# A fused AdaLN and ternary FFN kernel: the residual is read from DRAM a second time instead of being copied by ScalarE, and the input load moves to the top of the chunk

## The chip, the cores and the metric

The kernel runs on one core of a Trainium2 chip. The metric is the device time of one execution in microseconds, lower is better. Beside it stands the span of the profiled execution, which reaches from the first to the last instruction of the core.

## What is computed

```python
# conditional mixing of channels: per sample b an own 64 x 64 matrix
h = gelu(cond @ W0 + b0); h = gelu(h @ W1 + b1)
att = softmax(h @ W2 + b2)
agg_w = einsum('bk,koi->boi', att, weight); agg_b = att @ bias_k
y = einsum('boi,bih->boh', agg_w, x) + agg_b[:, :, None]
# feed-forward with ternary weights q(w) * mean|w|
gate = y @ deq(w_gate).T; up = y @ deq(w_up).T        # 1024 -> 2752
out = x + (gate * up) @ deq(w_down).T                 # 2752 -> 1024
```

x is 64 x 64 x 1024 in float32, that is 4096 tokens of 1024 values. The last line adds x itself: this is the residual.

## The kernel before

The 4096 tokens are worked through in eight chunks of 512 tokens, numbered 0 to 7. Chunk 0 runs together with the preparation of the weights (scales, ternary values, transposes, and the sums of weight blocks that a Strassen-like scheme needs, which are stored to DRAM as `wcomb`, `dcomb` and `wsub`). Chunks 1 to 7 follow one pattern. Chunk 1 (`FIRST`) and chunk 7 are written out, chunks 2 to 6 are a loop on each engine.

A chunk has eleven steps `p` on TensorE (`pairs`), each of which computes two 128-row blocks of gate and up as seven block products P1 to P7 (L971). In chunks 2 to 7, P2 and P5 are split once more (`inner_a` to `inner_d`, L983) and use extra weights, 128 KB for each of the two, that SyncE loads from `wsub` into `hi_r`/`sub` and `g_r` (`sub_load`, L603). Step 0 has only the first of the two. Twice in a chunk a group of down projections runs (`down_group`, L1089): group 0 before step 6, group 1 at the end. VectorE adds each of their banks, scaled, to `xr` (`output2`, L2016), which must hold the residual by then. After the last addition SyncE stores `xr` to the output (`store2`, L645), 256 KB at a time.

Within steps 2 to 5 of chunk c the input of chunk c+1 is mixed: `conv(c + 1, k)` (L742), two at a step, read `xa`, the 2 MB of x of chunk c+1, against `ablk`, the block-diagonal mixing matrices. The first of them stands in step 2, behind P1, `inner_a`, P4 and `inner_b`.

All loads of a chunk are issued from one queue, SyncE's, in a fixed order. SyncE runs down this list, and a wait stops all that is behind it:

```python
def chunk(c):
    if inners(c, 2):
        sub_third(c)          # waits for P2 of step 0, then loads the wsub blocks of step 2
    next_x(c)                 # ablk, xa and bias of chunk c+1
    pairs(c)                  # ring loads of wcomb (L597) and wsub blocks for the later steps
    next_pairs(c)
    store2(c)
    sp.wait_ge(s_dn, ...)
    down_load(0)              # 2240 KB of dcomb for the next chunk (L624)
```

`xr` gets its residual from ScalarE: `residual(c, t)` (L1219) copies a quarter of `xa` to `xr`, two quarters in step 0 and two in step 1, behind the copies of P1 and P6 that these steps need. Since `xa` may be overwritten only after that, `next_x` waits for all four copies (`s_xr`) besides the end of the chunk's own `conv` (`s_y`). The bias of chunk c+1 is loaded behind `xa`, 256 KB, one row spread over all partitions.

Of the kernel before, what the change touches and what calls it, by code (L numbers as in the profile page):

```python
# [5 lines left out]
def adaln_ternary_ffn(nc: bass.Bass, x, cond, w0, b0, w1, b1, w2, b2, wk, bias_k, w_gate, w_up, w_down, out):  # L6
# [15 lines left out]
    NT = TOK // P  # L22
    NC = B * C // TOK
# [7 lines left out]
    HB = H // TOK  # L31
# [59 lines left out]
    def sum_count(i):  # L91

        return on_act[i], sum((on_act if on_act[i] else on_dve)[:i + 1])
# [69 lines left out]
    with ctx:  # L163
        def sb(name, shape, dt):
            return ctx.enter_context(nc.sbuf_tensor(name, shape, dt))

        def sem(name):
            return ctx.enter_context(nc.semaphore(name))
# [9 lines left out]
        xa = sb("xa", [P, NT, H], f32)  # L178
        xr = sb("xr", [P, NT, H], f32)
# [212 lines left out]
        def inners(c, p):  # L392

            if isinstance(c, int) and c == FIRST or p == NPR:
                return ()
            return INNER[0:1 if p == 0 else NI]
# [46 lines left out]
        s_t = sem("s_t")  # L443
        s_te = sem("s_te")
        s_x = sem("s_x")
        s_xr = sem("s_xr")
        s_ablk = sem("s_ablk")
        s_bb = sem("s_bb")
        s_bbv = sem("s_bbv")
# [61 lines left out]
        s_res = [sem(f"s_res{t}") for t in range(NT)]  # L511
# [10 lines left out]
        s_st = [sem(f"s_st{t}") for t in range(NT)]  # L522

        xt = x.rearrange("(t b) c h -> t (b c) h", b=2)
# [6 lines left out]
        def _(sp):  # L531
            for dst, src in ((cond_sb, cond), (w0_sb, w0), (b0_sb, b0[:, None])):
                sp.dma_start(dst, src).then_inc(s_cond, 16)
            def load_x(c):

                sp.dma_start(xa[:, :, :], xt[bass.ds(c * NT, NT), :, :].rearrange("t p h -> p t h")).then_inc(s_x, 16)
# [8 lines left out]
            def load_bias(c):  # L545
                sp.dma_start(bbc[:, :], bias_row(c)).then_inc(s_bias, 16)

            last_in = {}
            for e, (n, _, _, s) in enumerate(loads):
                if e == 2:  # L550
                    load_x(0)
                if s in last_in:
# [3 lines left out]
                    else:  # L556
                        act, count = sum_count(summed.index(last_in[s]))
# [20 lines left out]
            sp.wait_ge(s_bst, 16)  # L578
            load_bias(1)

            def next_x(c):
                sp.wait_ge(s_xr, NT * c)
                sp.wait_ge(s_y, KH * c + KH)
                if isinstance(c, int) and c == FIRST:
                    sp.wait_ge(s_ad, 16)
                for h in range(2):
                    sp.dma_start(ablk[h * C:(h + 1) * C, :, h * C:(h + 1) * C],  # L587
                                 aggd[h * C:(h + 1) * C, bass.ds((c + 1) * NT, NT), :]).then_inc(s_abd, 16)
                load_x(c + 1)
                sp.wait_ge(s_ysc, KH * c + KH)  # L590
                load_bias(c + 1)
# [9 lines left out]
            def sub_load(c, p):  # L601
                for q, _ in enumerate(inners(c, p)):
                    sp.dma_start(sub_ring[q][p % 2], wsub[p, q]).then_inc(s_sub[p % 2], 16)  # L603

            def sub_third(c):
                sp.wait_ge(s_m2, NS * (c - FIRST) + 1)
                sub_load(c, 2)

            def next_pairs(c):
                if isinstance(c, int) and c == FIRST:  # L610
                    sp.wait_ge(s_subd, NI * NPR)
                for p, before in ((0, NPR - 1), (1, NPR), (2, NPR - 2)):
                    sp.wait_ge(s_m3, NS * (c - FIRST) + before + 1)
                    ring_load(p)
                if isinstance(c, int) and c == FIRST:
                    for i in range(2):
                        sp.wait_ge(s_subw[i], 16 * NI * (NPR // 2))
                sp.wait_ge(s_ulo, UP * FIRST + 2 * (c - FIRST) + 1)
                sub_load(c + 1, 0)
                sub_load(c + 1, 1)  # L620

            def down_load(g):
                dst = wd_flat[:, 0:GRP * PART].bitcast(f32).rearrange("p (q n) -> p q n", q=GRP)
                sp.dma_start(dst, dcomb[g * GRP:(g + 1) * GRP].rearrange("q p n -> p q n")).then_inc(s_wd, 16)  # L624

            def pairs(c):
                for p in range(RING, NS):
                    if p > RING and inners(c, p - 1):
                        sp.wait_ge(s_done[INNER[-1]], NS * (c - FIRST) + p - 2)
                        sub_load(c, p - 1)  # L630
                    sp.wait_ge(s_m3, NS * (c - FIRST) + p - RING + 1)
                    if isinstance(c, int) and c == FIRST:
                        sp.wait_ge(s_subd, NI * (p - RING + 1))
                    ring_load(p)
                    if p == NPR:
                        sp.wait_ge(s_dn, DN * FIRST + ND2 * (c - FIRST) + len(DOWN[0]))
                        down_load(1)

            def store2(c):
                for d, (what, j) in enumerate(DOWN[1]):  # L640
                    if d >= len(QUADS):
                        t, n = OUT[what][0] + j, OUT[what][1]
                        sp.wait_ge(s_o, DN * FIRST + ND2 * (c - FIRST) + len(DOWN[0]) + d + 1)
                        sp.sem_inc(s_turn_sp, 1)
                        sp.dma_start(ot[c * NT + t, :, n * TOK:(n + 1) * TOK],  # L645
                                     xr[:, t, n * TOK:(n + 1) * TOK]).then_inc(s_st[t], 16)
# [11 lines left out]
            down_load(0)  # L658

            def chunk(c):  # L660
                if inners(c, 2):
                    sub_third(c)
                next_x(c)
                pairs(c)
                next_pairs(c)
                store2(c)
                sp.wait_ge(s_dn, DN * FIRST + ND2 * (c - FIRST) + ND2)
                down_load(0)

            chunk(FIRST)  # L670
            with sp.Fori(FIRST + 1, NC - 1) as c:
                chunk(c)
            sub_third(NC - 1)
            pairs(NC - 1)
            store2(NC - 1)
# [520 lines left out]
        def _(act):  # L1196
# [15 lines left out]
                act.wait_ge(s_ysc, n + 1)  # L1212
                nc.scalar.copy(yp[:, k, 0, :], ys[:, k, :]).then_inc(s_yhi, 1)

            def residual(c, t):

                act.wait_ge(s_x, 16 * (c + 1))
                act.wait_ge(s_st[t], 16 * HB * c)
                nc.scalar.copy(xr[:, t, :], xa[:, t, :]).then_inc(s_xr, 1)  # L1219

            def raw_sum(i):
                e = summed[i]
                n = loads[e][0]
# [235 lines left out]
            def inner2(c, p):  # L1459
                n = len(inners(c, p))  # L1460
                act.wait_ge(s_ib, NPR * (c - FIRST - 1) + p + 1)
                nc.scalar.copy(uppers[:, 0:n, 0, :], lowers[:, 0:n, 0, :]).then_inc(s_e2, 1)
# [23 lines left out]
            def pairs(c, more):  # L1486
                for p in range(NS):
                    copy_p1(c, p)
                    if inners(c, p):
                        inner1(c, p)  # L1490
                    elif p < 2:
                        residual(c, 2 * p)
                        residual(c, 2 * p + 1)
                    if p:
                        gate21(c, p - 1)
                    if inners(c, p):
                        inner2(c, p)
                        inner3(c, p)
                    copy_p16(c, p)
                    if inners(c, p) and p < 2:  # L1500
                        residual(c, 2 * p)
                        residual(c, 2 * p + 1)
                    if more and p - 2 in range(KH // 2):
                        magnitudes(c + 1, 2 * (p - 2))
                        magnitudes(c + 1, 2 * (p - 2) + 1)
                    if p:
                        hi_blocks(c, p - 1)
                    copy_p167(c, p)
                    if p:
                        hi_sums(c, p - 1)  # L1510
                hi_rest(c)
                act.wait_ge(s_last, c - FIRST + 1)
                nc.scalar.copy(f_last[0], blocks4[0][:, 0:TOK]).then_inc(s_uhi, 1)
                if more:
                    hi_quarters(c + 1)
# [8 lines left out]
        def _(dve):  # L1524
# [476 lines left out]
            def output2(c, g, d):  # L2001
                done = DN * FIRST + ND2 * (c - FIRST) + g * len(DOWN[0])
                what, j = DOWN[g][d]
                t, n = OUT[what][0] + j, OUT[what][1]
                bank = DBANK[g][CHAIN[what]][j]
                dve.wait_ge(s_dn, done + d + 1)
                if g == 0 and d == 0:
                    dve.wait_ge(s_xr, NT * c)
                    dve.wait_ge(s_osc, c + 1)
                same = [e for e, (a, b) in enumerate(DOWN[g][:d]) if (OUT[a][0] + b, OUT[a][1]) == (t, n)]  # L2010
                if same:
                    dve.wait_ge(s_o, done + same[-1] + 1)
                elif g:
                    dve.wait_ge(s_o, done)
                cols = slice(n * TOK, (n + 1) * TOK)
                V.scalar_tensor_tensor(xr[:, t, cols], bank[:, :], osc[:, t:t + 1], xr[:, t, cols],  # L2016
                                       ALU.mult, ALU.add).then_inc(s_o, 1)
# [114 lines left out]
```

## Time and profile before

| | |
|---|---|
| median of 3 runs | 1733.4 us (1732.54 to 1737.3) |
| profiled execution | 1732.3 us, span 1730.3 us |
| TensorE busy | 1694.4 us, 98% of the span |
| VectorE busy | 1178.6 us, 68% |
| ScalarE busy | 682.1 us, 39% |
| mean granted TensorE clock | 0.995 |
| DRAM read, written | 176.63 MB, 34.68 MB |

Busy time counts only instructions that compute. The profiled execution took 2.0 us more than its span. The granted clock is the share of full speed that TensorE got: 1.00 is 2.4 GHz and 0.50 is 1.2 GHz.

### The profile page before, as it was taken

To read this page: it belongs to the slowest core of one execution; us is meant where nothing else is said; L and a number is where in the kernel's file an instruction comes from. 1 tells how busy PE (TensorE), PEld (TensorE's weight loads), DVE (VectorE), ACT (ScalarE), POOL (GpSimd) and SP (SyncE) were. 2 spreads that over 40 slices of the span, in tenths; PEclk is the share of its full clock that TensorE was granted. 3 is DMA by queue.
4 is the path that set the end of the run, shared out by engine and by line. 5 is a ranking of instruction groups with operands and counts; after the bars stand their busy time and mean duration, and the time that the engine had idled before them with its cause. 6 is when DMAs were issued, how large, how long until landed. Compare 5 with 4: busy or idle time off the path is not lost.

```text
span 1730.3 us, 35263 instructions
## 1 busy us (share of the span) xinstructions
PE 1694.4 (98%) x13784; PEld 1220.3 (71%) x13792; DVE 1178.6 (68%) x1960; ACT 682.1 (39%) x1281; POOL 89.3 (5%) x148
## 2 busy tenths in 40 slices
PE   6999999999999999999999999999999999999999
PEld 5554545977768686795957968587776868679594
DVE  6898895675766758566684766857576675766464
ACT  6887742322334234341433414343242423434140
POOL 0010004342000000000000000000000000000000
PEclk9999999999999999999999999999999999999999
DMA  8667626411333132430325302342133411332121
GB/s 342 248 243 254 215 104 224 141 62 50 143 111 139 56 114 86 166 106 28 120 104 169 103 31 104 120 164 83 51 142 110 141 56 58 136 136 93 40 99 49
DMA packets 80529, 213.62 MB, mean 123 GB/s; under 512 B 10704, under 2 KB 25616, under 8 KB 80240
## 3 DMA queue, kind: packets, MB, share of 16 engines
q1 hardware_dynamic: 76112, 193.23, 31.6%
q0 software_dynamic: 3664, 18.03, 2.7%
q8 instruction: 117, 1.92, 0.4%
q14 instruction: 44, 0.36, 0.1%
q10 hardware_dynamic: 592, 0.09, 0.0%
HBM read 176.63 MB, written 34.68 MB: 122 GB/s over the span
## 4 chain that ended last, share of the span: by engine, by line
PE 93%; DMA 3%; SPq 2%; ACT 1%; DVE 1%; issue 1%; ACTq 0%; DVEq 0%
PE ps L971 39%; PE ps L1089 25%; PE ps L742 17%; PE ps L983 10%; DMA xa<-in_x_dram 2%; PE ps L1048 2%; SPq L565 1%; DMA wuT<-in_L_ffn_w_gate_dram 1%; PE ps L848 1%; ACT xr L1219 1%; SPq L587 0%; DVE msk L1673 0%; DVE xa L1744 0%; DVE prod L1711 0%; ACT wdT L1282 0%
## 5 line engine op out<-in xcount | busy, mean ns | idle before, releaser
L971 PE MATMUL ps<-yp,wgT 128*128 128x256 f16 x3204 | 718.7, 273 | 1.0 <-issue 0.9
L971 PE MATMUL ps<-wuT,wgT 128*128 128x256 f16 x3204 | 718.5, 273 | 0.0
L1089 PE MATMUL ps<-wdT,inter 128*128 128x512 fp8e4 x1960 | 434.2, 379 | 0.5 <-DVE l L1610 0.2
L1089 PEld LDWEIGHTS ps<-wdT,inter 128*128 128x128 f16 x1960 | 191.3, 98 | 226.9
L971 PEld LDWEIGHTS ps<-yp,wgT 128*128 128x128 fp8e4 x3204 | 314.6, 98 | 38.7 <-issue 2.9
L971 PEld LDWEIGHTS ps<-wuT,wgT 128*128 128x128 fp8e4 x3204 | 314.5, 98 | 36.4
L2016 DVE SCALAR_TENSOR_TENSOR xr<-ps,osc,xr 128x512 f32<-128x512 f32 x210 | 156.9, 748 | 126.5 <-PE ps L1089 102.3
L1421 ACT COPY raw<-ps 128x512 f32<-128x512 f32 (+1 forms) x77 | 43.6, 567 | 307.3 <-PE ps L971 307.0
L1934 DVE TENSOR_TENSOR wdT<-ps,msk 128x512 f32<-128x512 f32 (+1 forms) x77 | 51.4, 667 | 78.9 <-PE ps L971 78.9
L742 PE MATMUL ps<-ablk,xa 128*128 128x128 f32 x512 | 71.9, 288 | 17.3 <-DMA xa<-in_x_dram 16.9
L1999 DVE TENSOR_TENSOR inter<-inter 128x1024 f16<-128x1024 f32 x70 | 85.3, 1218 | 0.0
L1943 DVE TENSOR_TENSOR ps<-p,ps 128x256 f32<-128x256 f32 x114 | 43.6, 426 | 56.7 <-ACT ps L1469 56.7
L742 PEld LDWEIGHTS ps<-ablk,xa 128*128 128x128 f32 x512 | 65.1, 200 | 20.3 <-issue 17.6
L1381 ACT CAST yp<-ys 128x1024 f16<-128x1024 f32 x49 | 48.4, 1042 | 72.7 <-DVE ys L1827 44.1
L742 PE MATMUL ps<-yp,wgT 128*128 128x512 f16 x336 | 76.0, 379 | 0.0
L983 PE MATMUL ps<-wuT,wgT 128*128 128x128 f16 x456 | 75.4, 219 | 0.0
L983 PE MATMUL ps<-yp,wgT 128*128 128x128 f16 x456 | 75.4, 219 | 0.0
L742 PE MATMUL ps<-yp,wuT 128*128 128x512 f16 x336 | 75.1, 379 | 0.0
L742 PE MATMUL ps<-wdT,inter 128*128 128x512 fp8e4 x336 | 73.8, 379 | 0.0
L1451 ACT CAST inter<-inter 128x1024 f16<-128x1024 f32 x70 | 73.4, 1048 | 0.0
L1435 ACT COPY raw<-ps 128x512 f32<-128x512 f32 (+1 forms) x77 | 43.5, 564 | 65.6 <-PE ps L971 65.6
L1443 ACT COPY inter<-ps 128x256 f32<-128x256 f32 x70 | 26.0, 372 | 107.6 <-PE ps L971 107.6
(273 smaller groups left out, 2311.7 us busy)
## 6 DMA issues: line engine op xcount, KB each, us to landing
wgT<-wcomb SPq DMA_DIRECT2D x70, 896.0 KB, 4.8
wdT<-dcomb SPq DMA_DIRECT2D x14, 2240.0 KB, 8.9
xa<-in_x_dram SPq DMA_DIRECT2D x8, 2048.0 KB, 8.5
out_dram<-xr SPq DMA_DIRECT2D x64, 256.0 KB, 2.0
wcomb<-xa POOLq DMA_DIRECT2D x17, 448.0 KB, 3.0
g_r<-wsub SPq DMA_DIRECT2D x54, 128.0 KB, 4.3
xr<-in_L_ffn_w_down_dram SPq DMA_DIRECT2D x9, 512.0 KB, 6.0
hi_r<-wsub SPq DMA_DIRECT2D x30, 128.0 KB, 3.6
```

The costliest lines, as they stand in the source:

```text
L742: return nc.tensor.matmul(o, l, r, start=start, stop=stop)
L971: last = nc.tensor.matmul(out, w, operand(i, OPERAND[what])[:, k, :], start=(start and h + k + i == 0), stop=(k == KQ - 1 and i == 1), ski ...
L983: last = nc.tensor.matmul(out, wk, inner_x(what, i, x)[:, k, :], start=(start and k + i == 0), stop=(k + i == 2), skip_group_check=True)
L1089: last = nc.tensor.matmul(bank[:, :], x, wd_block(p, BLOCK[what]), start=(what in ("P1", "P2", "P5") and q + i == 0), stop=(q == GRP - 1 a ...
L1381: nc.scalar.copy(operand(0, s), quarter(s)).then_inc(s_yhi, 1)
L1421: nc.scalar.copy(t1[:, 0:w], PB[p % 2][:, 0:w]).then_inc(s_t1, 1)
L1435: nc.scalar.copy(q67[:, 0:w], PB[p % 2][:, 0:w]).then_inc(s_q67, 1)
L1451: nc.scalar.copy(pair_parts(p, 0, 3, 4), sums).then_inc(s_hiS, 1)
L1934: V.tensor_tensor(rr[:, 0:w], PC[p % 2][:, 0:w], q6[p % 2][:, 0:w], ALU.add).then_inc(s_c12, 1)
L1943: last = V.tensor_tensor(inner_bank(p, what)[:, HALF:TOK].rearrange("p (a n) -> p a n", a=2), uppers[:, q], lowers[:, q, 1].unsqueeze(1).b ...
L1999: V.tensor_tensor(pair_parts(p, 1, 3, 4), sums, pair_parts(p, 0, 3, 4), ALU.subtract).then_inc(s_loS, 1)
L2016: V.scalar_tensor_tensor(xr[:, t, cols], bank[:, :], osc[:, t:t + 1], xr[:, t, cols], ALU.mult, ALU.add).then_inc(s_o, 1)
```

## The change

ScalarE's copies and their semaphore are removed. A new `load_res(c)` on SyncE's queue loads the same four quarters, 512 KB each, from x in DRAM to `xr`, each after the stores of that quarter of the chunk before have landed (`s_st[t]`). VectorE's outputs of group 0 wait for that load (`s_res[t]`). `next_x` loses the wait for the copies. `next_x` and `load_res` stand at the top of the chunk, ahead of `sub_third`. In chunk 7, which has no next chunk, only `load_res` is added, also ahead of `sub_third`.

```diff
+            def load_res(c):
+                for t in range(NT):
+                    sp.wait_ge(s_st[t], 16 * HB * c)
+                    sp.dma_start(xr[:, t, :], xt[c * NT + t]).then_inc(s_res[t], 16)
+
             def next_x(c):
-                sp.wait_ge(s_xr, NT * c)
                 sp.wait_ge(s_y, KH * c + KH)
...
             def chunk(c):
+                next_x(c)
+                load_res(c)
                 if inners(c, 2):
                     sub_third(c)
-                next_x(c)
                 pairs(c)
...
             with sp.Fori(FIRST + 1, NC - 1) as c:
                 chunk(c)
+            load_res(NC - 1)
             sub_third(NC - 1)
...
-            def residual(c, t):
-
-                act.wait_ge(s_x, 16 * (c + 1))
-                act.wait_ge(s_st[t], 16 * HB * c)
-                nc.scalar.copy(xr[:, t, :], xa[:, t, :]).then_inc(s_xr, 1)
...
                     if inners(c, p):
                         inner1(c, p)
-                    elif p < 2:
-                        residual(c, 2 * p)
-                        residual(c, 2 * p + 1)
...
                     copy_p16(c, p)
-                    if inners(c, p) and p < 2:
-                        residual(c, 2 * p)
-                        residual(c, 2 * p + 1)
...
                 if g == 0 and d == 0:
-                    dve.wait_ge(s_xr, NT * c)
                     dve.wait_ge(s_osc, c + 1)
...
                 elif g:
                     dve.wait_ge(s_o, done)
+                else:
+                    dve.wait_ge(s_res[t], 16 * (c + 1))
```

## Rows read from the trace of the kernel before

**Rows 1.** The page's chain that ended last, by engine and by line.

```profile
PE 93%; DMA 3%; SPq 2%; ACT 1%; DVE 1%; issue 1%; ACTq 0%; DVEq 0%
```

**Rows 2.** Waits of TensorE, whole span: total us, times, longest us.

```profile
PE ps L742 <- DMA xa<-in_x_dram: 16.9, 6, 3.8
```

**Rows 3.** The chain that ended last, 720 to 741 us (chunk 3): start us, us, what.

```profile
721.60 2.00 ACT xr L1219 x2
723.62 0.05 SPq L583
...
725.55 8.26 DMA xa<-in_x_dram
733.81 0.12 issue
733.93 1.58 PE ps L742 x8
...
739.82 1.75 PE ps L971 x16
```

**Rows 4.** The same chain, chunk 5, from its first input mixing on.

```profile
1149.12 1.15 PE ps L742 x8
...
1153.36 1.75 PE ps L971 x16
```

**Rows 5.** Busy time by stretch, chunk 3; last three columns: granted clock, DMA share, GB/s.

```profile
712.00:713.00 1.00, 1.00 (x14) 0.92 (x12) 0.65 (x1) 1.00 (x2) 0.00 (x0) 1.00 1.04 413
720.00:721.00 1.00, 1.00 (x13) 0.91 (x11) 0.68 (x3) 0.70 (x3) 0.00 (x0) 1.00 0.00 0
732.00:733.00 1.00, 0.00 (x0) 0.00 (x0) 0.37 (x2) 0.00 (x0) 0.00 (x0) 1.00 1.01 416
735.00:736.00 1.00, 1.00 (x7) 0.75 (x6) 0.13 (x1) 0.00 (x0) 0.00 (x0) 0.50 0.99 388
```

**Rows 6.** SyncE's DMA issues in order of time, chunk 3: start us, us.

```profile
706.40 0.43 SPq L624 DMA_DIRECT2D wdT<-dcomb  x1
712.34 0.33 SPq L603 DMA_DIRECT2D hi_r<-wsub  x1
...
723.89 1.48 SPq L587 DMA_DIRECT2D ablk<-aggd  x2
725.55 0.82 SPq L536 DMA_DIRECT2D xa<-in_x_dram  x1
726.57 0.35 SPq L546 DMA_DIRECT2D bbc<-biasd  x1
726.97 0.43 SPq L597 DMA_DIRECT2D wgT<-wcomb  x1
```

**Rows 7.** DMA issues of 700 to 740 us: count, KB each, us from issue to landing.

```profile
wdT<-dcomb SPq DMA_DIRECT2D x1, 2240.0 KB, 9.0
xa<-in_x_dram SPq DMA_DIRECT2D x1, 2048.0 KB, 8.3
wgT<-wcomb SPq DMA_DIRECT2D x1, 896.0 KB, 11.2
...
bbc<-biasd SPq DMA_DIRECT2D x1, 256.0 KB, 9.3
```

**Rows 8.** TensorE in order of time, first matmul of `inner_a` in step 2, chunk 3.

```profile
727.50 0.22 PE L983 MATMUL ps<-yp,wgT 128*128 128x128 f16 x1
```

**Rows 9.** The same two points of chunk 2, the issue of `dcomb` and that matmul.

```profile
499.39 0.43 SPq L624 DMA_DIRECT2D wdT<-dcomb  x1
...
520.12 0.22 PE L983 MATMUL ps<-yp,wgT 128*128 128x128 f16 x1
```

**Rows 10.** Start of the kernel: SyncE's issues, then busy time by stretch.

```profile
3.97 1.98 SPq L565 DMA_DIRECT2D wdT<-in_L_ffn_w_gate_dram  x3
10.38 7.08 SPq L565 DMA_DIRECT2D inter<-in_L_ffn_w_gate_dram  x7
...
8.00:24.00 16.00, 15.48 (x97) 13.38 (x98) 9.99 (x23) 9.90 (x20) 0.00 (x0) 1.00 1.02 409
```

**Rows 11.** Groups by line, ScalarE's copies: count, busy us, mean ns, idle before.

```profile
L1219 ACT COPY xr<-xa 128x1024 f32<-128x1024 f32 x28 | 27.9, 1048 | 0.0
```

**Rows 12.** VectorE in order of time, the first output of group 0 in chunk 3.

```profile
789.11 0.74 DVE L2016 SCALAR_TENSOR_TENSOR xr<-ps,osc,xr 128x512 f32<-128x512 f32 x1
```

More of the change, by code:

```diff
@@ L445, in adaln_ternary_ffn @@
         s_x = sem("s_x")
-        s_xr = sem("s_xr")
         s_ablk = sem("s_ablk")
```

## Prediction

> **What bounds the kernel now.** I read the page's chain of work that ended last first: TensorE holds 93% of it, DMA 3%, SyncE's queue 2% and ScalarE 1% [rows 1]. So the kernel is bound by TensorE's own work, and only time in which TensorE stands still or runs at half clock can be won. The list of TensorE's waits comes next. Its largest entry is the first input mixing, which waited for `xa` six times, 16.9 us in all, 3.8 us at most [rows 2]. Five of these are large, one in each of chunks 2 to 6 (3.4, 3.2, 3.8, 3.3 and 3.0 us in the waits of each chunk's stretch, sum 16.7 us); chunks 1 and 7 have none.
>
> The chain in order of time tells why `xa` is late. In chunk 3 ScalarE's last two residual copies run from 721.6 to 723.6 us, then SyncE's wait for them ends, it issues `ablk`, and at 725.55 us `xa`, which takes 8.26 us; the mixing starts at 733.93 us [rows 3]. Meanwhile the DMA engines were idle: 0 GB/s at 720 us [rows 5]. So the load is late because of its wait, not because the engines were full.
>
> The stall has a second price. After it the granted clock is 0.50 (1.2 GHz), where it was 1.00 (2.4 GHz) before and during most of it [rows 5]. From the first mixing to the end of the second, chunk 3 takes 739.82 - 733.93 = 5.89 us, chunk 5, which kept its full clock behind a like stall, 1153.36 - 1149.12 = 4.24 us [rows 3, 4]: 1.65 us lost. The same difference in chunks 4 and 6 is 1.65 us and in chunk 2 it is 1.37 us. Slow clock costs 3 x 1.65 + 1.37 = 6.3 us. All that the late `xa` costs is then 16.7 + 6.3 = 23.0 us.
>
> **The change part by part.**
>
> *Copies removed.* 28 copies of 1048 ns, 27.9 us [rows 11], leave ScalarE. It is no releaser of TensorE in any chunk from 1 to 7, so I take 0 from this. Bounds: 0 and, if the two copies of a step in chunk 1 hid a wait behind P6, a gain of about 2 us.
>
> *Wait removed and load moved.* `next_x` now runs behind `down_load(0)`, issued at 706.40 us in chunk 3 [rows 6]. From the end of SyncE's wait to the issue of `xa` it took 725.55 - 723.62 = 1.9 us [rows 3], so `xa` is issued near 708.9 us instead of 725.55. It is queued behind the 2240 KB of `dcomb`, which land 9.0 us after their issue [rows 7], that is at 715.4 us. With 5.1 us of transfer it is in by about 721.5 us, and the mixing wants it near 730.6 us (733.93 minus the 3.2 us stall and the release). The old stall goes, and its slow clock with it: a gain of 23.0 us if nothing else comes late.
>
> *What is now ahead of `sub_third`.* This is the step that decides. `sub_third` loads what `inner_a` of step 2 reads. Before, it was issued at 712.34 us [rows 6], as soon as P2 of step 0 was done, right behind `dcomb`, and had some 12 us to spare before 727.50 us [rows 8]. Now four residual loads (2048 KB in all), `xa` (2048 KB), `ablk` and the bias stand ahead of it, in one queue whose transfers land in the order of issue. I add up how long the queue needs, from the issue of `dcomb`:
>
> - `dcomb`: 9.0 us to landing, of which about 0.8 us is `sub_third`'s own data, which ran beside its tail: 8.2 us.
> - `ablk`: 128 KB in rows of 256 bytes. Before, it ran within the 1.48 us of its issues [rows 6]; 0.3 us (by bytes at 413 GB/s [rows 5]) to 2.0 us. I take 1.2.
> - `xa`: 2048 KB at 413 to 416 GB/s [rows 5] is 5.1 us. Upper bound 7.5 us, at the mean rate of `dcomb` (2.29 MB in 8.2 us, 280 GB/s).
> - bias: it landed at 726.57 + 9.3 = 735.9 us, `xa` at 725.55 + 8.3 = 733.9 us [rows 6, 7]: 2.0 us. Lower bound 0.7 us by bytes.
> - residual: 2048 KB as `xa`: 5.1 us, up to 7.5.
> - `sub_third`: 256 KB, 0.9 us; before, the like pair landed about that much behind the ring load at 726.97 + 11.2 = 738.2 us [rows 6, 7].
>
> Sum 22.5 us. `inner_a` starts 727.50 - 706.40 = 21.1 us after that issue in chunk 3 and 520.12 - 499.39 = 20.7 us in chunk 2 [rows 6, 8, 9]. With a mean need of 20.95 us and 0.12 us for the release [rows 3] the new stall is 1.7 us a chunk, five times: 8.5 us. Bounds: the low ends give 8.2 + 0.3 + 5.1 + 0.7 + 5.1 + 0.7 = 20.1 us, no stall; the high ends 8.2 + 2.0 + 7.5 + 2.0 + 7.5 + 0.9 = 28.1 us, a stall of 7.3 us. SyncE itself is no limit. The start of the kernel shows what it does with a long backlog: its issues of 512 KB grow from 0.66 to 1.0 us each while 409 GB/s move [rows 10]. An issue held up there is still served in turn.
>
> The rate of 413 to 416 GB/s is read from single microseconds and 409 GB/s from sixteen in a row [rows 5, 10]. The Trainium skill (DMA: Bandwidth & Descriptors, section Bandwidth) speaks against such a rate: it says that for transfers between HBM and SBUF the HBM side, about 358 GB/s a core, is what binds. By it the two 2 MB loads would take some 1.7 us more together, and the stall would be about 3.4 us. This trace does not agree with it, so my sum goes by the rows.
>
> *The clock behind the new stall.* I take no slow clock for a wait of 1.7 us. The rows show it behind waits of 3.0 us and more, and not even behind each of them [rows 3, 4]. Bounds: 0 and 1.65 us each, 8.2 us.
>
> *Chunks 1 and 7.* Chunk 1 has no `sub_third`. In chunk 7 the queue holds `dcomb` and the residual alone, 8.2 + 5.1 + 0.9 = 14.2 us against 21: nothing. The ring load of step 3 waits for P3 of step 0, near 722.7 us, and would land at about 731.5 us; before it landed at 738.2 us and nobody waited.
>
> *VectorE's new wait.* The residual is in by 728 us, and the first output of group 0 comes at 789.11 us [rows 12]. Cost 0, with 60 us of cover. The loads add 14.7 MB of DRAM traffic. Beyond its place in the queue I cost it at 0: TensorE was busy for all of the microsecond in which 413 GB/s moved [rows 5].
>
> Sum: 16.7 + 6.3 - 8.5 = 14.5 us less. The profiled execution took 1732.3 us, so 1717.8 us, and the median of the runs is 1.1 us above it: 1718.9 us.
>
> **The rivals.**
>
> *No new stall.* The queue drains a little faster than I add up, or `ablk` and bias overlap with their neighbours. Then all 23.0 us are won: 1710.4 us. For it: I am only 1.6 us over the need, and the two small loads, 3.2 us of my sum, move 0.9 us worth of bytes. Against it: the bias really held the queue for 2.0 us before.
>
> *The stall only changes its name.* The wait at `inner_a` is as long as the old one and slow clock follows as before. That needs the queue to take about 24.3 us, 1.8 us more than my sum, which loads at 350 GB/s give. Then 23.0 us are won and 5 x 3.4 + 6.3 = 23.3 us lost: 1733.7 us. It is in this mechanism that the rule above has its place, with that result.
>
> *Slower.* The queue runs at `dcomb`'s mean rate of 280 GB/s for the big loads, as two streams from x follow each other without a gap. At the high ends it takes 28.1 us, the stall is 7.3 us, and each is followed by slow clock: 5 x (7.3 + 1.65) = 44.8 us against 23.0, so 1755 us. It decides from 24.4 us on. For it: `dcomb` needed about 2 us to come up to full rate. Against it: that is a start, and the sustained rate in a long backlog was 409 GB/s [rows 10].
>
> *The change doesn't do what it says.* If `next_x` were held at the top by its other wait (`s_y`, done a chunk earlier), nothing would move. I see no way for this, and fold it into the case of no change.
>
> **How the numbers follow.** Chances: stall of 0.5 to 3 us moved to `inner_a`, 0.50; no stall, 0.20; the stall only renamed, 0.14; slower, 0.16. A measurement of this kernel can tell about 0.3%, 5 us. The likeliest case has its own range: a stall of 0.5 us gives 23.0 - 2.5 = 20.5 us and one of 3 us without slow clock 8 us, so 1713 to 1725 us. With the no-stall case below it and the renamed stall above it the range is 1709 to 1735 us, which leaves out the slower case. Faster by over 0.3%: 0.50 + 0.20 + 0.03 of the third = 0.73; within it 0.12; slower 0.15.
>
> **What would show it.** In the profile after: no wait of L742 for `xa`; `xa` issued within 3 us of `dcomb`; in chunks 2 to 6 a wait of L983 in step 2 for a `wsub` load, 1 to 2 us long, whose issue-to-landing time has grown from 3 us to 12 or more; mean granted clock nearly 1.00; no L1219. If the wait is over 3.4 us or the clock still falls, the sum of the queue is wrong and the time goes to 1733 us or beyond; if L983 never waits, it is 1710 us. A wait of VectorE at the first output of group 0 would break my claim of cover.

## The result, and the profile after

The changed kernel takes 1718.42 us in the median (1715.75 to 1721.8, 4 runs), the kernel before 1735.35 us beside it (1732.54 to 1737.93). The ratio is 0.9904, with a 95% interval of 0.9878 to 0.9930: faster, by 17 us. The forecast was 1718.9 us, a ratio of 0.9916 to the 1733.4 us of the section before. The profiled execution took 1718.81 us, span 1716.8 us, mean granted clock 0.997.

The first views are the page's shares of the chain that ended last, and below them the list of TensorE's waits (total us, times, longest us).

```profile
PE 90%; DMA 5%; SPq 2%; DVE 1%; issue 1%; ACT 1%; DVEq 0%; ACTq 0%
...
PE ps L988 <- DMA g_r<-wsub: 7.2, 5, 2.0
PE ps L752 <- DMA inter<-in_L_cond_b_dram: 4.2, 1, 4.2
PE ps L747 <- ACT msk L1236: 3.0, 1, 3.0
```

Where [rows 2] had 16.9 us of waiting for `xa`, the list has one wait of 0.3 us left, ahead of chunk 1. In its place stands a wait of the product matmuls for `g_r`, one of the two `wsub` blocks of step 2: five times, 7.2 us, once in each of chunks 2 to 6 (1.7, 1.4, 2.0, 1.2 and 0.9 us by each chunk's stretch). That is the new stall that the prediction put at 1.7 us a chunk. The DMA share of the chain went up from 3% [rows 1] to 5% although the kernel got faster: a chain credits the whole time of the load that released it, here some 15 us each, and not the wait alone.

SyncE's issues in chunk 3, in order of time (start us, us), answer to [rows 6]:

```profile
704.40 0.43 SPq L627 DMA_DIRECT2D wdT<-dcomb  x1
705.54 1.46 SPq L590 DMA_DIRECT2D ablk<-aggd  x2
707.18 0.47 SPq L535 DMA_DIRECT2D xa<-in_x_dram  x1
707.87 1.38 SPq L545 DMA_DIRECT2D bbc<-biasd  x1
709.52 1.92 SPq L583 DMA_DIRECT2D xr<-in_x_dram  x4
711.59 0.55 SPq L606 DMA_DIRECT2D hi_r<-wsub  x1
712.18 1.63 SPq L606 DMA_DIRECT2D g_r<-wsub  x1
720.63 0.37 SPq L600 DMA_DIRECT2D wgT<-wcomb  x1
```

`xa` is issued 2.8 us after `dcomb` instead of 19.2 us. The chain in order of time shows what became last instead (start us, us, what):

```profile
712.18 14.53 DMA g_r<-wsub
726.71 0.14 issue
726.85 1.05 PE ps L988 x16
```

The 128 KB of `g_r` were issued 7.8 us after `dcomb`, 1.5 us later than before, but need 14.53 us. They land 726.71 - 704.40 = 22.3 us after the issue of `dcomb`; the sum of the prediction was 22.5 us. Busy time by stretch (last three columns: granted clock, DMA share, GB/s) shows why: from 708 us on the DMA engines never paused.

```profile
708.00:714.00 6.00, 6.00 (x68) 5.50 (x67) 2.66 (x5) 1.70 (x4) 0.00 (x0) 1.00 1.00 374
715.00:720.00 5.00, 5.00 (x57) 4.57 (x55) 2.28 (x6) 2.04 (x6) 0.00 (x0) 1.00 1.02 401
721.00:726.00 5.00, 4.43 (x49) 3.80 (x46) 4.54 (x9) 2.90 (x4) 0.00 (x0) 1.00 1.04 398
```

The queue can be taken apart by its landings. These are the same issues of chunk 3 with KB and us from issue to landing (the second `ablk` load, issued at 706.39 us, and the last of the four `xr` loads, issued at 711.11 us):

```profile
wdT<-dcomb SPq DMA_DIRECT2D x1, 2240.0 KB, 9.6
ablk<-aggd SPq DMA_DIRECT2D x1, 64.0 KB, 8.4
xa<-in_x_dram SPq DMA_DIRECT2D x1, 2048.0 KB, 12.9
bbc<-biasd SPq DMA_DIRECT2D x1, 256.0 KB, 13.0
xr<-in_x_dram SPq DMA_DIRECT2D x1, 512.0 KB, 15.0
hi_r<-wsub SPq DMA_DIRECT2D x1, 128.0 KB, 13.2
```

Added to the starts above, `dcomb` lands 9.6 us after its issue, `ablk` at 10.4 us, `xa` at 15.7 us, the bias at 16.5 us, the last residual quarter at 21.7 us and `g_r` at 22.3 us. The order of landing is that of issue but for small loads: `hi_r`, issued behind all of the residual, landed at 20.4 us, 1.3 us ahead of its last quarter.

Slow clock came after one of the five waits, in chunk 4: this is its granted clock shortly behind the wait.

```profile
933.00:934.00 1.00, 1.00 (x6) 0.71 (x5) 0.00 (x0) 0.21 (x2) 0.00 (x0) 0.50 0.03 9
```

### The profile page after: what moved, and what is told of

Its sections match the earlier page's. It is cut to its first block, busy times and chain, and to the rows that moved or that the text cites. A ratio compares the mean times of both kernels' runs of the same rounds, so it can differ in the third digit from the quotient of the medians.

```text
span 1716.8 us, 35301 instructions
## 1 busy us (share of the span) xinstructions
PE 1692.5 (99%) x13792; PEld 1218.2 (71%) x13792; DVE 1178.6 (69%) x1960; ACT 656.3 (38%) x1253; POOL 90.5 (5%) x148
## 4 chain that ended last, share of the span: by engine, by line
PE 90%; DMA 5%; SPq 2%; DVE 1%; issue 1%; ACT 1%; DVEq 0%; ACTq 0%
PE ps L976 36%; PE ps L1094 25%; PE ps L747 18%; PE ps L988 9%; DMA g_r<-wsub 4%; PE ps L1053 2%; PE ps L853 1%; DMA xa<-in_x_dram 1%; SPq L583 0%; SPq L545 0%; SPq L590 0%; ACT msk L1236 0%; DVE xr L2010 0%; SPq L535 0%; DVE msk L1666 0%
## 5 line engine op out<-in xcount | busy, mean ns | idle before, releaser
L1911 DVE TENSOR_TENSOR wdT<-ps,raw 128x512 f32<-128x512 f32 (+1 forms) x77 | 51.3, 666 | 24.2 <-ACT raw L1434 24.2
```

Source lines behind the costliest of these rows:

```text
L1911: V.tensor_tensor(rr[:, TOK - w:TOK], PC[p % 2][:, 0:w], q67[:, 0:w], ALU.add).then_inc(s_c22, 1)
```

## The experiments

Each was run beside the kernel before on one chip, and its ratio is to that. "Wait" is TensorE's own wait for DMA in chunks 1 to 6 of the profiled execution.

**1. The wsub load first.** If only the order in the queue makes the new wait, putting this load back at the head must remove it, with all the rest of the change kept.

```diff
             def chunk(c):
-                next_x(c)
-                load_res(c)
                 if inners(c, 2):
                     sub_third(c)
+                next_x(c)
+                load_res(c)
...
+            sub_third(NC - 1)
             load_res(NC - 1)
-            sub_third(NC - 1)
```

> The changed kernel with the wsub load of step 2 back at the head of the chunk, and the input load and the residual loads behind it. Theory A (the stall of 7.2 us that the changed kernel shows at the first product of step 2 comes only from what stands ahead of that load in the queue): the input load is issued some 6 us later than in the changed kernel but still lands near 18 us after the chunk begins, before its use at 24 us; no wait of TensorE in chunks 2 to 6, no slow clock there, 7 to 9 us less than the changed kernel, about 1710 us and a ratio of 0.985 to the kernel before. Theory B (the queue as a whole carries too much, whatever the order): a wait of 1 to 2 us a chunk appears at the first input mixing or at the ring load of step 3 instead, 1718 us, ratio 0.990.

Measured: 1709.38 us (1707.79 to 1711.34), ratio 0.9865, interval 0.9846 to 0.9883. SyncE's issues in chunk 3, and the top of the list of waits, which holds no DMA wait of any chunk but the one at the start of the kernel:

```profile
702.28 0.97 SPq L627 DMA_DIRECT2D wdT<-dcomb  x1
708.63 0.33 SPq L606 DMA_DIRECT2D hi_r<-wsub  x1
...
711.38 0.98 SPq L535 DMA_DIRECT2D xa<-in_x_dram  x1
```

```profile
PE ps L752 <- DMA inter<-in_L_cond_b_dram: 4.2, 1, 4.2
PE ps L747 <- ACT msk L1236: 3.0, 1, 3.0
PE ps L747 <- DVE l L1617: 2.0, 1, 2.0
```

`xa` lands 8.6 us after its issue, at 720.0 us, and its first use comes at 726.88 us: it can afford being issued 9.1 us after `dcomb` instead of 2.8. Theory A holds, B falls.

**2. The residual loads alone behind the wsub load.** Here the input load stays at the top. The part left out swaps the two loads of chunk 7, as above.

```diff
             def chunk(c):
                 next_x(c)
-                load_res(c)
                 if inners(c, 2):
                     sub_third(c)
+                load_res(c)
...
```

> The changed kernel with the residual loads behind the wsub load of step 2, the input load still at the top. Theory A (the four residual loads, 5.1 us of queue, are what made the wsub load late): it lands near 17 to 18 us after the dcomb issue instead of 22.5, before its use at 21, so no wait, as in the version with the wsub load first; 1709 to 1710 us, ratio 0.9865. Theory B (the input load, ablk and bias ahead are enough): 1 us or more of wait a chunk stays, 1714 us or more.

Measured: 1709.66 us (1708.41 to 1710.17), ratio 0.9867 (0.9853 to 0.9882), and no wait either. The slowest `g_r` load of the kernel now takes 11.1 us from issue to landing instead of 15.1 us. In chunk 3, start us and us of the two issues, then KB and us from issue to landing of the second:

```profile
703.30 0.53 SPq L627 DMA_DIRECT2D wdT<-dcomb  x1
...
709.50 0.43 SPq L606 DMA_DIRECT2D g_r<-wsub  x1
```

```profile
g_r<-wsub SPq DMA_DIRECT2D x1, 128.0 KB, 10.8
```

It lands 17.0 us after `dcomb` was issued, 5.3 us earlier than in the changed kernel, where 2 MB more stood ahead of it. So the residual ahead was what made the load late: theory A holds, B falls.

**3. A longer queue.** The opposite: 512 KB more ahead of the wsub load.

```diff
...
                 load_res(c)
+                if not isinstance(c, int):
+                    sp.wait_ge(s_spare, 16 * (c - FIRST))
+                sp.dma_start(spare_x, xt[c * NT]).then_inc(s_spare, 16)
                 if inners(c, 2):
                     sub_third(c)
```

> The changed kernel with 512 KB more in SyncE's queue ahead of the wsub load of step 2: a quarter of x is copied once more, from DRAM to a DRAM tensor that nobody reads. Theory A (the stall is the time that the queue needs, whatever is in it): the wait grows by the time of those bytes, 1.3 us at 410 GB/s, up to 2.6 us if a copy within DRAM counts twice, so from 1.5 to about 2.8 to 4 us a chunk, 14 to 20 us in all, with slow clock behind some; 1725 to 1734 us, ratio 0.994 to 1.000. Theory C (the stall comes from the issue of the wsub load by SyncE, not from the queue behind it): the issue is only 0.5 us later, so 2 to 3 us more in all, ratio 0.992.

To have it beside the changed kernel on one chip, that was run again too:

> The changed kernel itself, unchanged, so that the three that follow can be compared with it on one chip. Theory A: ratio 0.990, a wait of 1 to 2 us at the first product of step 2 in each of chunks 2 to 6, 7 to 8 us in all.

Measured: the changed kernel 1720.09 us (1719.34 to 1725.37), ratio 0.9937 (0.9922 to 0.9951), wait 8.2 us; with the longer queue 1730.75 us (1726.29 to 1736.31), ratio 0.9990 (0.9977 to 1.0002), wait 14.7 us. The list of TensorE's waits, first of the changed kernel run again, then of the longer queue:

```profile
PE ps L988 <- DMA g_r<-wsub: 8.2, 5, 2.0
```

```profile
PE ps L993 <- DMA g_r<-wsub: 14.7, 5, 4.0
```

(14.7 - 8.2) / 5 = 1.3 us a chunk, and 512 KB at 400 GB/s take 1.3 us. The wait grew by the time of the added bytes (theory A), and a copy within DRAM counted once. This run alone doesn't rule out theory C, since SyncE also issued `g_r` later, 9.0 us after `dcomb` instead of 7.8 us. Experiment 2 does: there `g_r` was issued 6.2 us after `dcomb`, as early as in the kernel before (6.3 us), and yet took 10.8 us to land where it had taken 4.0 us, with `xa`, `ablk` and bias ahead of it. The medians differ by 10.7 us, of which the waits are 6.5; the profiled spans (1725.3 and 1717.4 us) by 7.9 us, with one more stretch of slow clock, about 1.7 us. A further 512 KB thus ate most of what the change had won.

**4. The bias out of the way.** The prediction gave the 256 KB bias load 2.0 us, more than its bytes.

```diff
                 load_x(c + 1)
-                sp.wait_ge(s_ysc, KH * c + KH)
-                load_bias(c + 1)
...
                 if inners(c, 2):
                     sub_third(c)
+                sp.wait_ge(s_ysc, KH * c + KH)
+                load_bias(c + 1)
```

> The changed kernel with the 256 KB bias load taken from ahead of the residual loads and put behind the wsub load of step 2. Theory A as in the prediction (the bias holds the queue for 2.0 us): the wait at the first product of step 2 falls by 2.0 us a chunk, to nothing in most, 1711 to 1713 us, ratio 0.987 to 0.989. Theory D (in a full queue the bias runs beside its neighbours and takes about 0.7 us): the wait falls by 0.7 us a chunk, to about 0.8 us, 1714 to 1717 us, ratio 0.990 to 0.992.

Measured: 1718.22 us (1712.34 to 1720.72), ratio 0.9909 (0.9892 to 0.9927), and in the list of waits:

```profile
PE ps L988 <- DMA g_r<-wsub: 3.1, 5, 0.8
```

That is 0.6 us a chunk, against 1.4 in the profile of the changed kernel and 1.6 in its second one: the bias took 0.8 to 1.0 us, near theory D's 0.7 us and not 2.0. The landings of the changed kernel say the same: in chunk 3 the bias came 0.8 us behind `xa`. The whole time is wide here. The profiled execution had a span of 1710.4 us and is the fastest of the runs, 6 us under their median, so the whole time can't weigh the two sizes and only the waits and landings do.

**5. The input load late again.** The copies stay removed and the residual comes from DRAM, but the input load is held back to where ScalarE's last copy had let it go.

```diff
             def chunk(c):
-                next_x(c)
-                load_res(c)
                 if inners(c, 2):
                     sub_third(c)
+                load_res(c)
+                sp.wait_ge(s_c12, NS * (c - FIRST) + 1)
+                next_x(c)
...
```

> The changed kernel with the wsub load and the residual loads first, and the input load held back until VectorE's addition for P3 of step 0, which ends close to where ScalarE's last residual copy ended in the kernel before. ScalarE's copies stay removed and the residual still comes from DRAM. Theory A (the lateness of the input load was what cost time): the input load is issued near 19 us into the chunk as before, TensorE waits about 3 us a chunk for it, 16 us in all, with slow clock behind most, and the time is that of the kernel before, 1733 us, ratio 0.997 to 1.002. Theory B (taking the copies off ScalarE gave part of the gain): ratio 0.993 to 0.996.

Measured: 1739.14 us (1733.78 to 1741.6), ratio 1.0037 (1.0023 to 1.0051). TensorE's waits, and the chain in chunk 3 as far as the mixing:

```profile
PE ps L748 <- DMA xa<-in_x_dram: 19.1, 7, 3.4
```

```profile
726.95 0.70 DVE wdT L1928
...
729.93 7.84 DMA xa<-in_x_dram
737.77 0.12 issue
737.89 1.15 PE ps L748 x8
```

`xa` is issued 19.3 us after `dcomb`, as in the kernel before (19.2 us). The whole gain is gone, though the copies are off ScalarE and the residual comes from DRAM. It is even 7 us worse than before, more than theory A's range allowed. 3.4 us of that are a wait in chunk 1, which this version holds back as well and which had none before. The profiled execution is the fastest of the ten and can't show the rest, but the mean granted clock of each run can: in the median 0.992 here and 0.995 for the kernel before beside it, which is about 5 us of 1735 us by my estimate. Theory A's mechanism holds, theory B falls.

**6. ScalarE's work put back.** Filler copies, as long as the removed ones and at their places.

```diff
...
+            def filler(c, p):
+                for i in range(7):
+                    if not (isinstance(c, int) and c == FIRST and p + i == 0):
+                        act.wait_ge(s_idle, 14 * (c - FIRST) + 7 * p + i)
+                    nc.scalar.copy(idle[:, :], ones[:, :]).then_inc(s_idle, 1)
...
+                    elif p < 2:
+                        filler(c, p)
...
                     copy_p16(c, p)
+                    if inners(c, p) and p < 2:
+                        filler(c, p)
```

> The changed kernel with as much copying put back on ScalarE as was removed, at the same places: 28 blocks' worth, seven copies of 128 x 128 for each two of the old ones, about 2.2 us each time, from a constant to a tile that nobody reads. Theory A (the copies cost nothing by themselves): same time as the changed kernel, within 2 us, ratio 0.990, and the waits of TensorE unchanged. Theory B (ScalarE's relief is part of the gain): 3 us or more slower than the changed kernel, with waits of TensorE for ScalarE in steps 0 and 1.

> The kernel with the filler copies on ScalarE once more, now on the same chip as the changed kernel. Theory A (the copies cost nothing by themselves; the 2.8 us more that it showed on another chip lie in the spread of the stall from execution to execution): within 3 us of the changed kernel. Theory B (they cost something): 3 us or more slower than it again.

Measured: 1721.21 us, ratio 0.9931 (0.9913 to 0.9948), and the second time, beside the changed kernel's 1720.09 us and 0.9937 (0.9922 to 0.9951), 1721.77 us and 0.9946 (0.9932 to 0.9960). The fillers were 98 copies of 299 ns, 29.3 us busy. No wait of TensorE for ScalarE appeared in steps 0 and 1; the waits for `g_r` were 8.5 and 9.0 us. The first time the kernel was 2.8 us slower than the changed kernel on another chip, on one chip 1.7 us. The intervals overlap: these runs show no cost of ScalarE's copies by themselves, but with four to six runs each they leave room for a few us. Experiment 7 narrows it.

**7. The kernel before, with the copies earlier.** If the late release was everything, the second read from DRAM is not needed at all. In chunks 2 to 7 ScalarE now makes two copies behind the copy of P6 and two behind that of P7, all in step 0.

```diff
                     copy_p16(c, p)
-                    if inners(c, p) and p < 2:
-                        residual(c, 2 * p)
-                        residual(c, 2 * p + 1)
+                    if inners(c, p) and p == 0:
+                        residual(c, 0)
+                        residual(c, 1)
...
                     copy_p167(c, p)
+                    if inners(c, p) and p == 0:
+                        residual(c, 2)
+                        residual(c, 3)
```

> The kernel before, with one thing changed: in chunks 2 to 7 ScalarE makes all four residual copies in step 0, two behind the copy of P6 and two behind the copy of P7, instead of two in step 1. No DRAM re-read, and SyncE's order is that of the kernel before. Theory A (only the late release of the input load cost time): the release comes at about 11 us into the chunk instead of 18, the input load lands near 21 to 22 us, its use is at 25 us, so the stall is gone, and with the wsub load of step 2 ahead no other takes its place: 20 to 23 us less than the kernel before, about 1713 us, ratio 0.987. Theory B (the DMA engines must have the second read in place of the copies to gain): little change, ratio 0.997 or more, and TensorE waits for ScalarE in step 1, whose copy of P1 comes late.

Measured: 1709.71 us (1708.5 to 1710.05), ratio 0.9865 (0.9845 to 0.9885). ScalarE in chunk 3, then SyncE's issues behind it:

```profile
707.34 0.59 ACT L1428 COPY msk<-ps 128x512 f32<-128x512 f32 x1 [0.44 <-PE ps L971]
707.82 2.00 ACT L1219 COPY xr<-xa 128x1024 f32<-128x1024 f32 x2
710.63 0.59 ACT L1435 COPY raw<-ps 128x512 f32<-128x512 f32 x1 [0.81 <-PE ps L971]
711.11 1.99 ACT L1219 COPY xr<-xa 128x1024 f32<-128x1024 f32 x2
713.00 0.59 ACT L1421 COPY raw<-ps 128x512 f32<-128x512 f32 x1
```

```profile
713.40 1.48 SPq L587 DMA_DIRECT2D ablk<-aggd  x2
715.06 0.47 SPq L536 DMA_DIRECT2D xa<-in_x_dram  x1
```

`xa` lands 7.8 us later, at 722.8 us, and is used from 727.12 us on. No wait remains in the chunks. Theory A holds, B falls. This version was run again beside the first experiment's on one chip:

> The kernel before with all four copies of ScalarE in step 0, once more, beside the next one on one chip: no wait of TensorE in chunks 2 to 7, 1709 to 1710 us, ratio 0.9865.

> The changed kernel with the wsub load of step 2 first, once more, beside the version above on one chip. Its 14.7 MB of additional DRAM reads are hidden, so the two should lie within 2 us of each other, 1709 to 1710 us, ratio 0.9865.

Measured: 1710.15 us (1708.5 to 1710.67), ratio 0.9862 (0.9843 to 0.9880), and 1708.61 us (1708.41 to 1709.61), ratio 0.9858 (0.9840 to 0.9876). The two can't be told apart, and each beats both kernels. One of them has ScalarE's copies and the other the second read of x from DRAM, so the two cost the same within about 2 us. Against the kernel before, these four measurements win 22.3 to 24.8 us, and 23.0 us was all that the late `xa` was put at, which leaves little for a cost of either.

## Why the prediction was right

*What bounds the kernel.* Right: the late input load cost a wait in chunks 2 to 6, and nothing else that the change removes mattered. Experiment 5 gives the gain back by that one delay. Experiment 7 wins 22.3 and 23.2 us by that one release, where all that the late `xa` costs was put at 23.0 us.

*Copies removed: 0.* Right within some 2 us (experiments 5, 6 and 7).

*The moved load: all of the old stall.* Right. No wait for `xa` is left in chunks 1 to 7, and the 16.7 us of waiting are gone.

*The queue ahead of `sub_third`.* The deciding step was right in kind and in its sum, 22.5 us forecast and 22.3 us measured, and the stall, 8.5 us forecast, was 7.2 us in one profile and 8.2 us in the other. Its terms were less good, and that the sum came within 0.2 us is partly luck. By the landings of chunk 3 the bias took 0.8 us instead of 2.0. This was made up for by `dcomb` and `ablk`, which needed 10.4 us together instead of 9.4. The other terms were near: `xa` 5.3 us instead of 5.1, the residual 5.2 instead of 5.1, the wsub pair 0.6 instead of 0.9. In chunks 2 to 6 the bias landed 0.7 to 1.0 us behind `xa`, and `g_r` 22.0 to 22.9 us after `dcomb` was issued. With the other terms as forecast and the bias at 0.8 us the sum would have been 21.3 us and the stall 0.5 us a chunk. "Transfers land in the order of issue" was too strict, as `hi_r` shows, but `g_r`, the load waited for, did land behind all that was issued before it.

The rate that the Trainium skill names as binding (DMA: Bandwidth & Descriptors, section Bandwidth, about 358 GB/s a core) was exceeded here too: the trace held 398 to 401 GB/s for five microseconds at a time, twice. The same section of the Trainium skill measured 425 GB/s for 16 MB with the pair's other core idle, so it does not speak against the rate as flatly as the prediction had it. At 358 GB/s the estimate for the two 2 MB loads would be 1.5 us more, not 1.7.

*The clock: 0 behind the new stall.* Nearly right: one slow stretch, about 1.7 us, in the first profile, and none in chunks 2 to 6 of the second. Before there were four. That the one came behind a wait of 2.0 us was outside what the rows before had shown.

*Chunks 1 and 7, and VectorE's new wait: 0.* Right. No wait of TensorE for a load stands in those stretches, and the first output of group 0 comes at 783.41 us in chunk 3, while the residual had landed by 726.1 us. Chunk 1, from its issue of `dcomb` to the next chunk's, took 205.27 us in both kernels, and the last part, from chunk 7's issue on, 195.9 us in both.

*The sum.* Forecast 14.5 us. The spans give 1730.3 - 1716.8 = 13.5 us: 16.7 + 6.3 us removed, 7.2 + 1.7 us added is 14.1 us. From the issue of `dcomb` at the start of chunk 2 to that at the start of chunk 7 the kernel before took 1534.44 - 499.39 = 1035.05 us and the changed one 1520.94 - 500.60 = 1020.34 us, 14.7 us less. That is 0.6 us more than the waits and the slow clock account for. The whole span gained 1.2 us less, lost ahead of chunk 1, in the preparation, which the change leaves alone. The ratio of the runs, 0.9904 at first and 0.9937 on another chip, lies on both sides of the forecast 0.9916.

*The rivals.* "No new stall" and "the stall only changes its name" did not come, but both are close by: 2 MB behind the wsub load instead of ahead of it make the first (experiment 2), and 512 KB more bring the kernel almost back to its old time (experiment 3). "Slower" rested on 280 GB/s for the big loads, and they ran at about 400.

## What to carry to other kernels

When an issue is moved up in an in-order queue, add up everything that now stands ahead of each load behind it, and compare the landing with the instant of its use. For the big loads the bytes at the sustained rate were right to 0.2 us each; the start of the queue and the bias were off by 1.0 and 1.2 us, against a margin of 1.6 us between a stall and none. Before replacing a copy by a transfer, ask whether the cost was the copy or the moment at which it let something go: here a larger gain came from ending the copies 7 us earlier in the chunk, without reading 14.7 MB twice. Loads whose use is far off (the residual, 60 us) belong behind those whose use is near.

## What the runs showed of the hardware that was not expected

The same small transfer cost the queue twice as much in one place as in another. The bias, 256 KB from one row, landed 2.0 us behind `xa` in the kernel before [rows 6, 7], 1.7 to 2.0 us in chunks 2 to 6. In the changed kernel it was 0.7 to 1.0 us. The queue was not short in either: before, the ring load of 896 KB was issued 0.4 us behind the bias, now the residual. The rows of the two microseconds around the landing of `xa` differ (last three columns: granted clock, DMA share, GB/s), first before, then after:

```profile
733.00:734.00 1.00, 0.07 (x1) 0.07 (x1) 0.00 (x0) 0.00 (x0) 0.00 (x0) 1.00 1.08 194
734.00:735.00 1.00, 1.00 (x7) 1.00 (x8) 0.00 (x0) 0.00 (x0) 0.00 (x0) 0.75 0.99 196
```

```profile
719.00:720.00 1.00, 1.00 (x12) 0.89 (x11) 0.51 (x2) 0.47 (x1) 0.00 (x0) 1.00 0.98 389
720.00:721.00 1.00, 1.00 (x17) 0.96 (x15) 0.37 (x1) 0.00 (x0) 0.00 (x0) 1.00 1.06 426
```

Both times the DMA engines were busy throughout, but before they moved half as much. Why was not shown.

Slow clock does not follow from the length of a wait alone. With the longer queue TensorE waited five times for 2.6 to 4.0 us, and one of the five, the longest, was followed by 0.50. In the changed kernel it was one of 2.0 us; in its second profile one of 2.0 us was not followed by it. Kernels with waits also spread more from run to run, 1726.29 to 1736.31 us in experiment 3 against 1708.41 to 1709.61 us for a version without any. The clock goes along with this spread: the fastest of those twelve runs had a mean granted clock of 0.996 and the slowest 0.992, and 0.004 of 1730 us is 7 us, by my estimate, of the 10 us between them.

SyncE's issues took longer behind a long queue. That of the bias took 0.35 us before [rows 6] and 1.38 us after. No harm from it showed: in chunk 5 `g_r` was issued 8.0 us after `dcomb` and landed at 22.2 us, in chunk 3 it was issued at 7.8 us and landed at 22.3 us.
